# A two-layer graph attention kernel: in layer 1 the edges of the next block are made by GpSimd and the row maxima stay in PSUM

## The chip, the cores and the metric

The kernel runs on one core of one Trainium2 chip. The metric is the device time of one execution in microseconds (us); lower is better. Before the change it is 3500.31 us, the median of 3 runs (3499.39 to 3500.57). TensorE does the matmuls (PE in the profile; PEld are its weight loads), VectorE (DVE) and ScalarE (ACT) the elementwise work, GpSimd (POOL) and SyncE (SP) mainly issue transfers.

## The reference, cut to what matters

There are three attention layers over N = 8192 nodes with C = 64 channels and one 8192x8192 integer adjacency: one in the first residual block, two in the second. Each does, for every row of the adjacency, a masked softmax and a weighted sum of features:

```
e = leaky_relu(u[:, None] + v[None, :] (+ c), 0.2)
scores = where(adj > 0, e, -9e15)
att = softmax(scores, axis=1)
h = elu(att @ features ...)
...
x = layernorm(x + gnn0(x, adj))          # kernel layer 0
x = layernorm(x + gnn1(x, adj))          # kernel layers 1 and 2, then an MLP over [x, h1, h2]
```

The adjacency is read as integers once; the kernel turns it into a byte mask, keeps that mask in device memory and reads it again in layers 1 and 2.

## The kernel before, in words

The program calls its three attention layers l = 0, 1, 2. Each layer is worked in NB = 16 blocks of BI = 512 rows of the adjacency (they lie along the free axis, so everything is transposed), and each block in NT = 64 tiles of 128 columns (they lie on the partitions). The code is written out by hand for each engine: each of them runs the same loop over blocks and tiles, and semaphores hold them together. There is no scheduler; what stands at a tile index `t` in an engine's loop is issued after that engine's work on tile t.

For tile j of a block:
- DVE, `start_scores` (L1156): writes max(ua + v8col[j], cb) into one of ES = 5 score banks `eps` of PSUM. `ua` (128x512) holds the rows' u minus their maxima, `cb` (128x512) the negative maxima, both in SBUF; `v8col[j]` is a [128, 1] operand. It waits until the bank's last user, ACT five tiles ago, is done.
- PE, `mask_scores` (L754): adds a large negative number to the bank where the mask `nt` says "no edge".
- ACT, `probs` (L577): exp of the bank into `prob`.
- PE, `sums` (L798): sums prob times features into the bank `acc`, two tiles per group in layers 1 and 2.

At fixed tile indices two more pieces of work are threaded into the loop of block b.

The tail of block b-1, T_TURN to T_Y (tiles 8 to 35): PE turns the sums into the bank `misc`, DVE divides, applies the elu and makes the features (L1071 to L1099, ending in `s_h`), PE makes the next layer's products, ACT copies them out, and DVE adds them to the running output at tile 35 (L1121, signalled by `s_y`). GpSimd then issues two stores: `u_d` (L521) and `xy_d` (L524). SP loads `xin` for the next tail and the masks of a later block once the `xy_d` store is complete.

The head of block b+1: the kernel wants the largest v among each row's neighbours. `make_edges` (L1004, DVE) turns a quarter of the mask (16 tiles, 128x2048 int32) into 0/1 in FP8 by an exclusive-or with EDGE_FLIP, four times a block, at tiles T_XOR = 29, 32, 40, 41, into two buffers `edges`. PE counts edges by level of v (`count_edges`, L765, tiles 35 and 43), ACT copies the counts out (tile 45), PE turns them (`turn_counts`, L774, tile 47), DVE finds the maxima (`head`, L1022 to L1048, tiles 51 to 53; fourteen instructions, of which the first waits for the turned counts). PE turns the maxima (L841) and spreads them over all partitions into `misc` (L846, tile 57), ACT copies `misc` to `cb` (`rows_out`, L641), and DVE makes the next `ua` (`add_u`, L1162, tile 63).

PSUM has eight banks: five `eps`, `acc`, `den` and `misc`. In layers 0 and 2 `den` sums denominators; in layer 1 it is unused, since the denominator comes out of a turned sum. All tail and head steps share `misc`.

In layer 1 GpSimd has the two stores of each block and nothing else. The 5 buffers `stage`, in which the adjacency lands in layer 0, are unused in layers 1 and 2.

Of the kernel before, what the change touches and what calls it, by code (L numbers as in the profile page):

```python
# [16 lines left out]
P = 128  # L17
# [22 lines left out]
EDGE_FLIP = 0x38383838  # L40
LEVELS = float(HB * LV - 2)
# [63 lines left out]
def build(nc, x, adj, ent, W0, a0, W12, lin_w, lin_b, attn, mlp_w, mlp_b, out):  # L105
    with ExitStack() as ctx:
# [92 lines left out]
        miscb = misc[:, :].bitcast(BF16)  # L199
# [30 lines left out]
        s_xor = sem("edges_made")  # L230
        s_oneh = sem("levels_on_columns")
# [261 lines left out]
        def _(pool):  # L493
# [43 lines left out]
        def _(act):  # L537
# [60 lines left out]
            def columns_out(l, b):  # L598
                act.wait_ge(s_htt, blk(l, b) + 1)
                nc.scalar.activation(ht[0:C, :], misc[0:C, :], ACT.Copy).then_inc(s_hte, 1)  # L600

            def products_out(l, b, i):

                act.wait_ge(s_om, 4 * blk(l, b) + i + 1)
                if i < 2:
                    v = misc[:, 0:2 * WC].rearrange("p (r w) -> p r w", w=WC)
# [19 lines left out]
                elif l < 2:  # L626

                    act.wait_ge(s_ust, 16 + 16 * blk(l, b))
                    nc.scalar.activation(urow[:, :], misc[0:RT, 0:P], ACT.Copy).then_inc(s_oe, 2)

            def counts_out(l, b):
                act.wait_ge(s_hist, MV * (blk(l, b) + 1))
                nc.scalar.activation(hs[:, :], misc[:, :], ACT.Copy).then_inc(s_hse, 1)  # L633

            def maxima_out(l, b, par):
                act.wait_ge(s_mt, blk(l, b) + 1)
                nc.scalar.activation(mrow[0:3, par, :], miscb[0:3, 0:BI], ACT.Copy).then_inc(s_mte, 1)  # L637
# [18 lines left out]
            for l in range(NLAYER):  # L656
                counts_out(l, 0)
                maxima_out(l, 0, 0)
                rows_out(l, 0, 0)

                def body(b, par, head, tail):
                    for t in range(NT):
# [8 lines left out]
                        if b == 0 and l == 1 and t == T_FSUM:  # L671
                            act.wait_ge(s_fs1, 1)
                            nc.scalar.activation(acc_s[0:C, 0:P], misc[0:C, 0:P], ACT.Copy).then_inc(s_fs1e, 1)
                        if b == 0 and t == T_FSUM + 4:
                            act.wait_ge(s_fsum, l + 1)
                            nc.scalar.activation(fsum[:, :], misc[:, 0:CE], ACT.Copy).then_inc(s_fsume, 1)
# [4 lines left out]
                        if head and t == T_ROWS:  # L681
# [9 lines left out]
        def _(pe):  # L691
# [66 lines left out]
            def count_edges(l, b, m):  # L758

                n = MV * blk(l, b) + m  # L760
                pe.wait_ge(s_xor, n + 1)
                for k in range(MT // 4):
                    for s in range(4):
                        j = 4 * k + s
                        mm = nc.tensor.matmul(misc[s * HB:(s + 1) * HB, :], oneh[:, m * MT + j, :],  # L765
                                              half_block(edges[:, n % 2, :], m, j), start=(m == 0 and k == 0),
# [11 lines left out]
            def feature_sum(l, j):  # L778
                if l == 1:
                    mm = nc.tensor.matmul(misc[0:C, 0:P], feat[:, 1, j, 0:C], ones[:, :], start=(j == 0),  # L780
# [4 lines left out]
                mm = nc.tensor.matmul(misc[:, 0:CE], ones[:, :], feat[:, l % 2, j, :], start=(j == 0),  # L785
# [52 lines left out]
            def turn_maxima(l, b):  # L838
                pe.wait_ge(s_split, blk(l, b) + 1)
                for r in range(RT):  # L840
                    mm = nc.tensor.transpose(miscb[0:3, r * P:(r + 1) * P], parts[:, r, 0:3], identb[:, :])  # L841
                mm.then_inc(s_mt, 1)

            def spread_maxima(l, b, par):
                pe.wait_ge(s_mte, blk(l, b) + 1)
                nc.tensor.matmul(misc[:, :], onesb[:, :], mrow[:, par, :], start=True, stop=True).then_inc(s_cb, 1)  # L846

            def tail_step(l, b, t):
                if t == T_TURN:
# [4 lines left out]
                    for r in range(RT):  # L854
                        if l == 1:
                            mm = nc.tensor.matmul(misc[:, r * CE:(r + 1) * CE], acc_s[:, r * P:(r + 1) * P],
                                                  turnw[:, :], start=True, stop=True)
                            continue
                        nc.tensor.matmul(misc[:, r * CE:r * CE + C], acc_s[:, r * P:(r + 1) * P], halves[:, 0:C],  # L859
                                         start=True, stop=True)  # L860
                        mm = nc.tensor.matmul(misc[:, r * CE + C:(r + 1) * CE], den_s[:, r * P:(r + 1) * P],  # L861
                                              halves[:, C:CE], start=True, stop=True)
                    mm.then_inc(s_gt, 1)
                if t == T_HT:
                    for r in range(RT):
                        mm = nc.tensor.transpose(misc[0:C, r * P:(r + 1) * P], hn[:, r, :], ident[:, :])  # L866
# [426 lines left out]
```

## Time and profile before

| | |
|---|---|
| median of 3 runs | 3500.31 us |
| the profiled execution | 3499.27 us |
| its span | 3497.5 us |
| PE busy | 3203.8 us (92%) |
| DVE busy | 2873.2 us (82%) |
| ACT busy | 2269.0 us (65%) |
| POOL busy | 114.3 us (3%) |
| granted TensorE clock, mean | 0.983 |

A busy share says what part of the span an engine had an instruction in flight. Matmuls are pipelined and their ends are modelled, so a PE that reads 94% busy may still be waiting for a little in front of each instruction. Layer 0 lasts until about 1450 us of the span, layer 1 from there to about 2385 us, layer 2 to the end. In a timeline view the columns are the start in us, the duration of the row in us, engine, line, operation, output and inputs with their shapes, how many instructions the row joins, and in brackets how long the engine had been idle and what released it.

### The profile page before, as it was taken

Reading aid. Unit: us, or ns where it says so; the run is one execution under the profiler, and the core shown is the slowest. Engines: PE = TensorE matmul, PEld = TensorE weight load, DVE = VectorE, ACT = ScalarE, POOL = GpSimd, SP = SyncE. Lnnn points to the kernel's source line nnn. Section 1 sums busy time; section 2 is a strip of 40 time slices with the busy share of each in tenths; the row PEclk is TensorE's granted clock in tenths of the full one; section 3 lists DMA queues with packets and bytes.
Section 4 is the critical chain, followed back from the end, with each engine's and each line's share of the span. In section 5 each row is a group of like instructions: output and inputs, shape, how many; then the busy total and the mean of one; then the engine's idle time right before and its main releaser. Section 6 shows DMA issues by size and latency. Waiting matters only on the chain. (4 is left out here: it accounts for less than half of the span.)

```text
span 3497.5 us, 58252 instructions
## 1 busy us (share of the span) xinstructions
PE 3203.8 (92%) x22959; PEld 1152.7 (33%) x22959; DVE 2873.2 (82%) x5283; ACT 2269.0 (65%) x3933; POOL 114.3 (3%) x138
## 2 busy tenths in 40 slices
PE   1679999999999999799999999988999999999998
PEld 0323333333333333333333333334333333333333
DVE  5468888888888875699999999986888888888886
ACT  0247766676776666377777787773666666666665
POOL 0000000000000000000000000000000000000000
PEclk9989999999999999899999999998999999999999
DMA  8999999999999951222222222112111211221210
GB/s 253 283 348 346 341 329 347 336 333 340 343 333 341 333 180 54 85 85 97 76 100 73 100 73 101 72 61 85 69 72 64 90 71 57 86 82 57 85 33 7
DMA packets 414116, 578.71 MB, mean 165 GB/s; under 512 B 294402, under 2 KB 315010, under 8 KB 389266
## 3 DMA queue, kind: packets, MB, share of 16 engines
q1 hardware_dynamic: 409458, 564.40, 50.2%
q0 software_dynamic: 4384, 10.59, 1.0%
q8 instruction: 180, 2.95, 0.4%
q14 instruction: 94, 0.77, 0.1%
HBM read 430.10 MB, written 77.69 MB: 145 GB/s over the span
## 5 line engine op out<-in xcount | busy, mean ns | idle before, releaser
L1156 DVE SCALAR_TENSOR_TENSOR eps<-ua,v8col,cb 128x512 f32<-128x512 f32 x2800 | 1971.3, 754 | 376.3 <-ACT prob L577 238.9
L577 ACT ACTIVATE prob<-eps,v2col 128x512 f32<-128x512 f32 x2560 | 1628.4, 688 | 692.2 <-PE eps L754 678.9
L798 PE MATMUL acc<-prob,feat 128*64 128x512 f32 x5120 | 1303.3, 605 | 6.6 <-ACT acc_s L585 6.6
L754 PE MATMUL eps<-nt,nbig 128*64 128x512 fp8e4 (+2 forms) x6542 | 994.3, 384 | 114.4 <-DVE eps L1156 110.4
L754 PEld LDWEIGHTS eps<-nt,nbig 128*64 128x64 bf16 (+2 forms) x6542 | 329.8, 104 | 956.0 <-DVE eps L1156 612.5
L798 PEld LDWEIGHTS acc<-prob,feat 128*64 128x64 f32 x5120 | 326.2, 137 | 397.9 <-issue 215.0
L577 ACT ACTIVATE mi<-eps,v2col 128x512 f32<-128x512 f32 x512 | 328.0, 686 | 156.7 <-PE eps L754 152.7
L995 DVE TENSOR_SCALAR mi<-stage 128x1024 uint8<-128x1024 int32 x512 | 352.2, 689 | 62.9 <-DMA stage<-in_adj_dram 62.5
L807 PE MATMUL den<-prob,ones 128*32 128x512 f32 x3072 | 397.0, 604 | 0.0
L798 PE MATMUL acc<-mi,feat 128*64 128x512 f32 x1024 | 264.8, 597 | 0.0
L1004 DVE TENSOR_SCALAR edges<-nt 128x2048 int32<-128x2048 int32 x192 | 234.2, 1220 | 31.1 <-PE misc L765 16.3
L765 PE MATMUL misc<-edges,oneh 128*32 128x512 fp8e4 x3072 | 190.8, 390 | 70.6 <-DVE edges L1004 55.8
L564 ACT ACTIVATE eps<-ub,v8col 128x512 f32<-128x512 f32 x272 | 189.4, 696 | 0.0
L807 PEld LDWEIGHTS den<-prob,ones 128*32 128x32 f32 x3072 | 67.1, 108 | 301.0 <-issue 301.0
L765 PEld LDWEIGHTS misc<-edges,oneh 128*32 128x32 bf16 x3072 | 85.0, 98 | 198.3 <-issue 81.1
L807 PE MATMUL den<-mi,ones 128*32 128x512 f32 x1024 | 123.1, 598 | 0.0
L751 PE MATMUL eps<-mrow,onesb 128*32 128x512 bf16 (+1 forms) x800 | 106.5, 379 | 0.0
L633 ACT ACTIVATE hs<-misc 128x512 f32<-128x512 f32 x48 | 28.3, 589 | 93.8 <-PE misc L765 93.8
L798 PEld LDWEIGHTS acc<-mi,feat 128*64 128x64 f32 x1024 | 68.2, 137 | 54.4 <-issue 20.2
L878 PEld LDWEIGHTS misc<-wcat,ht 65*128 65x128 f32 x384 | 52.5, 198 | 77.8 <-issue 49.5
L637 ACT ACTIVATE mrow<-misc 3x512 bf16<-3x512 bf16 x48 | 28.1, 586 | 76.3 <-PE misc L841 76.3
L878 PE MATMUL misc<-wcat,ht 65*128 65x130 f32 (+1 forms) x384 | 69.8, 306 | 6.5 <-ACT pj L624 4.5
(159 smaller groups left out, 1407.1 us busy)
## 6 DMA issues: line engine op xcount, KB each, us to landing
stage<-in_adj_dram SPq DMA_DIRECT2D x512, 512.0 KB, 6.5
nt<-nt_d SPq DMA_DIRECT2D x128, 1024.0 KB, 5.2
nt_d<-nt SPq DMA_DIRECT2D x64, 1024.0 KB, 7.2
ub<-u_d SPq DMA_DIRECT2D x48, 256.0 KB, 5.2
xy_d<-xin POOLq DMA_DIRECT2D x32, 256.0 KB, 3.3
xin<-xy_d SPq DMA_DIRECT2D x32, 256.0 KB, 2.9
nt<-mi SPq DMA_TRANSPOSE x256, 7.2
xin<-in_x_dram SPq DMA_DIRECT2D x16, 128.0 KB, 6.3
```

Source lines behind the costliest of these rows:

```text
L564: nc.scalar.activation(eps[:, j % ES, :], ub[:, par, :], ACT.Relu, bias=v8col[:, j:j + 1], scale=1.0 - ALPHA).then_inc(s_filla, 1)
L577: nc.scalar.activation(weights(l, j), eps[:, j % ES, :], ACT.Exp, bias=v2col[:, j:j + 1]).then_inc(s_p, 1)
L633: nc.scalar.activation(hs[:, :], misc[:, :], ACT.Copy).then_inc(s_hse, 1)
L751: nc.tensor.matmul(et[c:c + cols, :], onesb[:, c:c + cols], mrow[:, par, :], start=False, stop=False, skip_group_check=True, tile_position ...
L754: mm = nc.tensor.matmul(et[c:c + cols, :], nbig[:, c:c + cols], edge, start=False, stop=True, skip_group_check=True, tile_position=(0, c))
L765: mm = nc.tensor.matmul(misc[s * HB:(s + 1) * HB, :], oneh[:, m * MT + j, :], half_block(edges[:, n % 2, :], m, j), start=(m == 0 and k == 0),
L798: mm = nc.tensor.matmul(acc[h:h + C, :], feat[:, l % 2, j, 0:C], weights(l, j), start=(k == 0), stop=(k == NT // 2 - 1))
L807: mm = nc.tensor.matmul(den[32 * i:32 * i + 32, :], ones[:, 0:32], weights(l, QUAD * k + i), start=(k == 0), stop=(k == NT // QUAD - 1))
L878: mm = nc.tensor.matmul(misc[:, r * WC + w:(r + 1) * WC], ht[:, (2 * i + r) * P:(2 * i + r + 1) * P], wcat[:, l, w:WC], start=True, stop=True)
L995: dv.tensor_scalar(out, src, 0, ONE8, ALU.is_le, ALU.mult).then_inc(s_mask, 1)
L1004: dv.tensor_scalar(edges[:, n % 2, :].bitcast(I32), nt[:, b % 2, m, :].bitcast(I32), EDGE_FLIP, None, ALU.bitwise_xor).then_inc(s_xor, 1)
L1156: dv.scalar_tensor_tensor(eps[:, j % ES, :], ua[:, par, :], v8col[:, j:j + 1], cb[:, par, :], ALU.add, ALU.max).then_inc(s_fill, 1)
```

## The change

Five things change, all for layer 1.

1. The edges of blocks 1 to 15 are made by GpSimd and no longer by DVE. Each quarter is made in EDGE_PARTS = 4 instructions of 128x1024 16-bit elements, as 0x3838 minus the mask, where DVE did one exclusive-or of 128x2048 int32.
2. Quarters 0 and 1 go to the two `edges` buffers, quarters 2 and 3 to the first four `stage` slots, so each quarter of a block has its own buffer.
3. In GpSimd's program the first two quarters stand ahead of a wait for the tail's features (`s_h`), the other two behind it, and the stores `u_d` and `xy_d` of the tail behind both.
4. The maxima stay in PSUM: the blocks of layer 1 use `misc` and `den` in turn (`max_bank`), `start_scores` and `add_u` read the bank, and ACT's copy to `cb` is gone in this layer. The tail and head steps use the other bank (`work_bank`).
5. The waits on the counters follow: PE waits for `s_edge`, and `s_cbe` (now without layer 1's copies) is counted by `copied`.

Block 0 of layer 1 and all of layers 0 and 2 keep their edges on DVE.

```diff
+EDGE_PARTS = 4
+EARLY_EDGES = 2
@@
+        edges1 = stage[:, 0:4, :].rearrange("p s w -> p (s w)").bitcast(U8).rearrange("p (m w) -> p m w", m=2)
@@
+        def max_bank(b):
+            return (misc, den)[b % 2][:, :]
+        def work_bank(l, b):
+            return max_bank(b + 1) if l == 1 else misc[:, :]
+        def by_pool(l, b):
+            return l == 1 and b > 0
+        def edge_buffer(l, b, m):
+            return edges1[:, m - 2, :] if by_pool(l, b) and m >= 2 else edges[:, m % 2, :]
@@ GpSimd
-            for l in range(NLAYER):
-                for b in range(NB):
-                    tail(l, b)
+            def make_edges(b, m):
+                n = MV * blk(1, b) + m
+                sl, count = landed(1, b, m)
+                pool.wait_ge(sl, count)
+                if b > 1:
+                    pool.wait_ge(s_hist, n - MV + 1)
+                elif m < 2:
+                    pool.wait_ge(s_hist, n - 1)
+                w = MT * BI // EDGE_PARTS
+                for i in range(EDGE_PARTS):
+                    nc.gpsimd.tensor_scalar(edge_buffer(1, b, m)[:, i * w:(i + 1) * w].bitcast(U16),
+                                            nt[:, b % 2, m, i * w:(i + 1) * w].bitcast(U16), -1.0,
+                                            float(EDGE_FLIP & 0xffff), ALU.mult, ALU.add).then_inc(s_edge, 1)
+
+            for b in range(NB):
+                tail(0, b)
+            for b in range(NB):
+                for m in range(MV if b < NB - 1 else 0):
+                    if b > 0 and m == EARLY_EDGES:
+                        pool.wait_ge(s_h, blk(1, b - 1) + 1)
+                    make_edges(b + 1, m)
+                if b > 0:
+                    tail(1, b - 1)
+            tail(1, NB - 1)
+            for b in range(NB):
+                tail(2, b)
@@ ScalarE
-                        if head and t == T_ROWS:
+                        if head and t == T_ROWS and l != 1:
                             rows_out(l, b + 1, 1 - par)
@@ TensorE, count_edges
-                pe.wait_ge(s_xor, n + 1)
+                if by_pool(l, b):
+                    pe.wait_ge(s_edge, EDGE_PARTS * (MV * (b - 1) + m + 1))
+                else:
+                    pe.wait_ge(s_xor, MV * (NB + 1 + b if l == 2 else blk(l, b)) + m + 1)
@@ VectorE
+            def maxima(l, b, par):
+                return max_bank(b) if l == 1 else cb[:, par, :]
-                dv.scalar_tensor_tensor(eps[:, j % ES, :], ua[:, par, :], v8col[:, j:j + 1], cb[:, par, :],
+                dv.scalar_tensor_tensor(eps[:, j % ES, :], ua[:, par, :], v8col[:, j:j + 1], maxima(l, b, par),
@@
-                            for m in range(MV):
+                            for m in range(0 if by_pool(l, b + 1) else MV):
                                 if t == T_XOR[m]:
                                     make_edges(l, b + 1, m)
```

DVE's program in a middle block of layer 1, before: from the tiles behind the features to the first instruction of the head.

```order
L1156 SCALAR_TENSOR_TENSOR eps<-ua,v8col,cb 128x512 x9
L1004 TENSOR_SCALAR edges<-nt 128x2048
L1156 SCALAR_TENSOR_TENSOR eps<-ua,v8col,cb 128x512 x3
L1004 TENSOR_SCALAR edges<-nt 128x2048
L1156 SCALAR_TENSOR_TENSOR eps<-ua,v8col,cb 128x512 x3
L1121 TENSOR_TENSOR xin<-xin,pj 128x4x64
L1156 SCALAR_TENSOR_TENSOR eps<-ua,v8col,cb 128x512 x5
L1004 TENSOR_SCALAR edges<-nt 128x2048
L1156 SCALAR_TENSOR_TENSOR eps<-ua,v8col,cb 128x512
L1004 TENSOR_SCALAR edges<-nt 128x2048
L1156 SCALAR_TENSOR_TENSOR eps<-ua,v8col,cb 128x512 x10
L1022 TENSOR_SCALAR he<-misc 128x128
```

The same place in DVE's program of the change (`den` is here the bank that holds the block's maxima, `misc` the work bank):

```order
L1212 SCALAR_TENSOR_TENSOR eps<-ua,v8col,den 128x512 x15
L1174 TENSOR_TENSOR xin<-xin,pj 128x4x64
L1212 SCALAR_TENSOR_TENSOR eps<-ua,v8col,den 128x512 x16
L1074 TENSOR_SCALAR he<-misc 128x128
L1075 SCALAR_TENSOR_TENSOR hx<-he,kstep 128x128
L1076 TENSOR_TENSOR hx<-hx,he 128x128
L1077 TENSOR_REDUCE kmax<-hx 128x4
```

The four `edges` instructions are gone from between the scores, and the scores read a PSUM bank in place of `cb`.

GpSimd's program before, from the last block of layer 0 into layer 1: each block of layer 1 has its two stores. The names in brackets are the semaphores that a row waits for: `next_products_out` is `s_oe`, `output_sums_done` is `s_y`.

```order
L517 TENSOR_TENSOR rstd<-mom,half 128x4 [waits variance_done]
L521 DMA u_d<-urow 4x128 [waits next_products_out]
L524 DMA xy_d<-xin 128x4x128 [waits output_sums_done]
L521 DMA u_d<-urow 4x128 [waits next_products_out]
L524 DMA xy_d<-xin 128x4x128 [waits output_sums_done]
```

GpSimd's program of the change, one block of layer 1 (`mask_loaded0` to `mask_loaded7` are the landings of the mask quarters, 0 to 3 of even and 4 to 7 of odd blocks, `edges_counted` is `s_hist`, `features_done` is `s_h`):

```order
L564 TENSOR_SCALAR edges<-nt 128x1024 [waits edges_counted,mask_loaded0]
L564 TENSOR_SCALAR edges<-nt 128x1024 x3
L564 TENSOR_SCALAR edges<-nt 128x1024 [waits edges_counted,mask_loaded1]
L564 TENSOR_SCALAR edges<-nt 128x1024 x3
L564 TENSOR_SCALAR stage<-nt 128x1024 [waits edges_counted,mask_loaded2,features_done]
L564 TENSOR_SCALAR stage<-nt 128x1024 x3
L564 TENSOR_SCALAR stage<-nt 128x1024 [waits edges_counted,mask_loaded3]
L564 TENSOR_SCALAR stage<-nt 128x1024 x3
L543 DMA u_d<-urow 4x128 [waits next_products_out]
L546 DMA xy_d<-xin 128x4x128 [waits output_sums_done]
```

Sixteen instructions now stand ahead of a block's stores, eight of them behind the wait for the features.

## Rows read from the trace of the kernel before

**Rows 1.** Busy time by stretch: layer 1, layer 2, one block of layer 1. Columns: stretch, length, each engine's busy us, clock, DMA share, GB/s.
```profile
1450.00:2385.00 935.00, 860.28 (x5433) 311.82 (x5432) 861.23 (x1523) 698.92 (x1222) 20.62 (x32) 0.99 0.24 86
2385.00:3497.50 1112.50, 1093.97 (x7641) 401.23 (x7641) 904.38 (x1694) 697.49 (x1167) 40.60 (x32) 0.98 0.17 63
1615.75:1672.61 56.86, 53.41 (x340) 19.11 (x338) 53.98 (x95) 44.09 (x78) 1.28 (x2) 1.00 0.24 89
```

**Rows 2.** Timeline of DVE in that block.
```profile
1615.75 9.37 DVE L1156 SCALAR_TENSOR_TENSOR eps<-ua,v8col,cb 128x512 f32<-128x512 f32 x14
...
1632.27 0.43 DVE L1099 SCALAR_TENSOR_TENSOR hn<-hn,z 128x256 f32<-128x256 f32 x1
...
1638.58 1.22 DVE L1004 TENSOR_SCALAR edges<-nt 128x2048 int32<-128x2048 int32 x1
1639.71 2.08 DVE L1156 SCALAR_TENSOR_TENSOR eps<-ua,v8col,cb 128x512 f32<-128x512 f32 x3
...
1644.82 0.42 DVE L1121 TENSOR_TENSOR xin<-xin,pj 128x256 f32<-128x256 f32 x1
...
1659.73 0.29 DVE L1022 TENSOR_SCALAR he<-misc 128x128 int32<-128x128 int32 x1
```

**Rows 3.** Groups by line, 1505 to 2295 us: count, busy us, mean ns, idle before.
```profile
L1156 DVE SCALAR_TENSOR_TENSOR eps<-ua,v8col,cb 128x512 f32<-128x512 f32 x890 | 609.0, 753 | 31.5 <-ACT prob L577 30.1
...
L1004 DVE TENSOR_SCALAR edges<-nt 128x2048 int32<-128x2048 int32 x56 | 68.3, 1219 | 0.0
...
L1071 DVE SCALAR_TENSOR_TENSOR g<-fsum,emp,misc 128x65 f32<-128x65 f32 x56 | 11.9, 275 | 0.0
...
L1162 DVE SCALAR_TENSOR_TENSOR ua<-ub,cb 128x512 f32<-128x512 f32 x13 | 8.9, 685 | 0.0
...
L1099 DVE SCALAR_TENSOR_TENSOR hn<-hn,z 128x256 f32<-128x256 f32 x14 | 6.0, 426 | 0.5
...
L1030 DVE SCALAR_TENSOR_TENSOR ns<-vm,gst,vucol 128x4 f32<-128x4 f32 x14 | 3.1, 223 | 0.5
```

**Rows 4.** Timeline of PE in that block, in order of time.
```profile
1634.99 1.02 PE L798 MATMUL acc<-prob,feat 128*64 128x512 f32 x4
...
1645.37 1.03 PE L798 MATMUL acc<-prob,feat 128*64 128x512 f32 x4
...
1648.62 1.02 PE L798 MATMUL acc<-prob,feat 128*64 128x512 f32 x4
...
1649.91 1.02 PE L798 MATMUL acc<-prob,feat 128*64 128x512 f32 x4
...
1657.66 1.02 PE L798 MATMUL acc<-prob,feat 128*64 128x512 f32 x4
...
1660.05 1.08 PE L798 MATMUL acc<-prob,feat 128*64 128x512 f32 x4
```

**Rows 5.** Timeline of SP: loads behind the tail's store.
```profile
1648.79 0.37 SPq L385 DMA_DIRECT2D xin<-xy_d  x1
1649.22 23.61 SPq L437 DMA_DIRECT2D nt<-nt_d  x4
```

**Rows 6.** DMA issues, 1648 to 1656 us: KB each, median us to landing.
```profile
nt<-nt_d SPq DMA_DIRECT2D x2, 1024.0 KB, 6.5
```

**Rows 7.** Groups by line on POOL, whole span.
```profile
L499 POOL MEMSET mrow<- 128x1024 bf16 x1 | 1.0, 951 | 0.1
...
L502 POOL TENSOR_SCALAR_AFFINE_SELECT ident<-ident 128x128 f32<-128x128 f32 x1 | 0.3, 290 | 0.2 <-POOL halves L499 0.2
```

**Rows 8.** Timelines of POOL and DVE in layer 0; last, POOL's group in layer 1.
```profile
513.22 1.10 POOL L521 DMA_DIRECT2D u_d<-urow  x1 [13.59 <-ACT urow L629]
...
513.54 0.69 DVE L995 TENSOR_SCALAR mi<-stage 128x1024 uint8<-128x1024 int32 x1
...
L521 POOL DMA_DIRECT2D u_d<-urow x14 | 7.3, 518 | 837.2 <-ACT urow L629 837.2
```

More of the change, by code:

```diff
@@ L311, in freed, with copied @@
             return tile(l, b, last) - NT + 1
+        def copied(l, b):
+            return b + 1 if l == 0 else NB + b + 1
         def den_blocks(l, b):
@@ L599, in columns_out @@
                 act.wait_ge(s_htt, blk(l, b) + 1)
-                nc.scalar.activation(ht[0:C, :], misc[0:C, :], ACT.Copy).then_inc(s_hte, 1)
+                nc.scalar.activation(ht[0:C, :], work_bank(l, b + 1)[0:C, :], ACT.Copy).then_inc(s_hte, 1)
             def products_out(l, b, i):
@@ L764, in count_edges @@
                         j = 4 * k + s
-                        mm = nc.tensor.matmul(misc[s * HB:(s + 1) * HB, :], oneh[:, m * MT + j, :],
-                                              half_block(edges[:, n % 2, :], m, j), start=(m == 0 and k == 0),
+                        mm = nc.tensor.matmul(wb[s * HB:(s + 1) * HB, :], oneh[:, m * MT + j, :],
+                                              half_block(eb, m, j), start=(m == 0 and k == 0),
                                               stop=(m == MV - 1 and k == MT // 4 - 1), skip_group_check=True,
@@ L779, in feature_sum @@
                 if l == 1:
-                    mm = nc.tensor.matmul(misc[0:C, 0:P], feat[:, 1, j, 0:C], ones[:, :], start=(j == 0),
+                    mm = nc.tensor.matmul(work_bank(1, 0)[0:C, 0:P], feat[:, 1, j, 0:C], ones[:, :], start=(j == 0),
                                           stop=(j == NT - 1))
@@ L784, in feature_sum @@
                     return
-                mm = nc.tensor.matmul(misc[:, 0:CE], ones[:, :], feat[:, l % 2, j, :], start=(j == 0),
+                mm = nc.tensor.matmul(work_bank(l, 0)[:, 0:CE], ones[:, :], feat[:, l % 2, j, :], start=(j == 0),
                                       stop=(j == NT - 1))
@@ L845, in spread_maxima @@
                 pe.wait_ge(s_mte, blk(l, b) + 1)
-                nc.tensor.matmul(misc[:, :], onesb[:, :], mrow[:, par, :], start=True, stop=True).then_inc(s_cb, 1)
+                nc.tensor.matmul(work_bank(l, b - 1), onesb[:, :], mrow[:, par, :], start=True, stop=True).then_inc(s_cb, 1)
             def tail_step(l, b, t):
+                wb = work_bank(l, b + 1)
                 if t == T_TURN:
@@ L927, in body @@
                             pe.wait_ge(s_fs1e, 1)
-                            nc.tensor.matmul(misc[:, 0:CE], acc_s[0:C, 0:P], turnw[0:C, :], start=True,
+                            nc.tensor.matmul(work_bank(1, 0)[:, 0:CE], acc_s[0:C, 0:P], turnw[0:C, :], start=True,
                                              stop=True).then_inc(s_fsum, 1)
@@ L1003, in make_edges @@
                     dve.wait_ge(s_hist, n - 1)
-                dv.tensor_scalar(edges[:, n % 2, :].bitcast(I32), nt[:, b % 2, m, :].bitcast(I32), EDGE_FLIP, None,
+                dv.tensor_scalar(edge_buffer(l, b, m).bitcast(I32), nt[:, b % 2, m, :].bitcast(I32), EDGE_FLIP, None,
                                  ALU.bitwise_xor).then_inc(s_xor, 1)
@@ L1071, in tail_aggregate @@
                     ins = dv.scalar_tensor_tensor(g[:, r, :], fsum[:, :], emp[:, par, r:r + 1],
[L1072 removed]
+                                                  work_bank(l, b + 1)[:, r * CE:(r + 1) * CE], ALU.mult,
+                                                  ALU.add)
                 step(ins, seq, at + 1)
```

50 lines of the change are left out of this document (27 added, 23 removed).

## Prediction

> **What bounds the kernel now.** I read the busy time by stretch first. In layer 1, the only layer that the change touches, 935 us hold 860 us of PE and 861 us of DVE; in layer 2 PE is busy for 1094 of 1112 us and DVE for 904 [rows 1]. So layer 2 is PE's alone, and layer 1 is shared. One block of layer 1 takes 56.86 us with 53.41 us of PE, 53.98 of DVE and 44.09 of ACT [rows 1]. A busy PE is not PE at its peak, so the two have to be counted by their spacing.
>
> DVE, from its timeline in the block: 14 scores in a row take 9.37 us with the last one 0.75 long, so they follow each other every (9.37 - 0.75) / 13 = 0.663 us [rows 2], shorter than the 753 ns of one, since they overlap [rows 3]. 64 of them are 42.4 us. One `edges` instruction moves the next score by 1639.71 - 1638.58 = 1.13 us [rows 2], four are 4.5 us. DVE idles ahead of scores for 31.5 us over 14 blocks [rows 3], 2.3 a block. The rest of 56.86 is tail and head, 7.7 us.
>
> PE, from its timeline: where nothing holds it, a group of two tiles (masks and sums) takes 1649.91 - 1648.62 = 1.29 us [rows 4]; 32 groups are 41.3. A group that DVE holds takes 2 x 0.663 = 1.33. Counting two quarters of edges adds 1648.62 - 1645.37 - 1.29 = 1.96 us, twice a block, 3.9. Turning the counts adds 1660.05 - 1657.66 - 1.29 = 1.10. The middle of the tail, six groups, takes 1645.37 - 1634.99 = 10.38, which is 2.6 over six plain ones [rows 4]. Turning the sums, and the two steps of the maxima together, I put at 1.1 each like the counts. The sum is 51.1 us.
>
> So DVE needs 54.6 us of the 56.9, PE 51.1: DVE is the bound of layer 1, by a little.
>
> **The change part by part.** Edges off DVE: 4.5 us a block, in 15 blocks (those whose next block is in layer 1 as well). DVE then needs 50.1, PE 51.1, and PE becomes the bound. The two don't meet smoothly: DVE is at most five banks ahead, that is five tiles or 3.3 us, and its work in the head comes as one piece. I add 1.2 us for what PE still waits: 52.3 us a block if GpSimd disturbs nobody. That is 4.5 us saved in each of 15 blocks, 68 us.
>
> Maxima in PSUM: ACT loses one 128x512 copy a block, ACT has 12 us of a block idle [rows 1], nothing. At the layer's start one such copy leaves the path, some 0.6 us. What matters is whether a score that reads PSUM in place of `cb` takes longer. Two instructions of one form with SBUF operands give the slope: (685 - 426) / 256 = 1.01 ns an element and 167 ns fixed. The 65-element one that reads `misc`, with a [128, 1] operand, has 275 - 66 = 209 fixed; the 4-element one that reads SBUF, also with a [128, 1] operand, 223 - 4 = 219 [rows 3]. So reading PSUM costs between 10 ns less than SBUF and, if the whole of 209 - 167 is its doing, 42 ns more. I take nothing, since the pair with the same kind of operand is the nearer; the upper end is 64 x 0.042 = 2.7 us a block.
>
> The rule of the Trainium skill that speaks against this edit is in "VectorE: DVE Perf Modes", on the errata: a VectorE instruction with its source in PSUM has 120 fixed cycles where SBUF has 58. By it each score would lose an estimated 62 cycles, 0.065 us, and a block 4.1 us, nearly all that the edges give. The rows above don't show such a difference, though none reads and writes PSUM at once.
>
> GpSimd's time for a part: the trace has no `tensor_scalar` of POOL. The nearest rows are a memset of 128x1024 16-bit elements, 951 ns, and a 128x128 select with input and output, 290 ns [rows 7]. Below, 0.95 us is the floor; above, the select's whole time scaled by eight, 2.3 us. I take 1.03 us with the gap to the next, because the select read and wrote and its 290 ns are mostly fixed. A quarter of a block is then 4.1 us and half a block 8.2.
>
> Late half: the features end at 1632.27 + 0.43, 17 us into the block [rows 2]. Eight parts end at 25.2. The output sum at tile 35 comes at 29.1 now [rows 2] and, two edges earlier, near 26.8, so the stores behind it wait for nothing new. PE counts these quarters at tile 43, over 8 us later still. Free.
>
> Early half: it stands at a block's beginning in the program, but what it waits for is the landing of the masks, and SP asks for those behind the store of `xin`. In the block shown the output sum is at 1644.82, SP's load of `xin` at 1648.79, the first two mask quarters go out at 1649.22 [rows 2, 5] and land 6.5 us later [rows 6], at 1655.7. GpSimd has nothing else by then, so the early half runs there, 10.9 us after the output sum, and not at the next block's beginning. The head begins at 1659.73 [rows 2], 4.0 us behind that start, when PE has turned the counts. With DVE further ahead of PE, the output sum moves some 1.3 us forward against it: 5.3 us. So of 8.2 us, 2.9 still lie in front when the head begins, three parts.
>
> Do they disturb each other? Of the head's fourteen instructions all but `he` (it reads PSUM) and the reduction work on SBUF tiles alone. POOL's store at 513.22 took 1.10 us, where the same takes 518 ns in layer 1; DVE had one 0.69 us instruction in flight from 513.54 to 514.23, and POOL's ended 0.09 behind it [rows 8]. So an instruction of one engine can hold the other's for its whole length. In "SBUF — State Buffer" the Trainium skill says so as a rule (section "SBUF: two separate sides"): DVE and GpSimd share a pair of ports, DVE takes it with two SBUF inputs or in a two-port mode, and whoever has it keeps it for the whole instruction. The rows show POOL held by DVE; that DVE is held by POOL is the other half of the rule and stands in no row.
>
> I take the scores, which now have an operand in PSUM, to be clear of the parts, and the tail lies between the halves. The head's twelve instructions within SBUF I take to be held: each can wait for the part in flight, and three parts cost 0.5 + 1.0 + 1.0 = 2.5 us, less 0.3 that the PE waits anyhow, 2.2 us. PE has only four tiles in hand there, and the head without this already uses them up, so 2.2 us are late on PE too. Bounds: nothing (no holding, or the early half over in time) and all eight parts in the head, 8 us.
>
> **Sum.** 52.3 + 2.2 = 54.5 us a block in place of 56.86, 2.36 saved, in 15 blocks 35 us; with the layer's start 35.6. Against the profiled execution of 3499.3 us that is 3463.7, and the median stands 1 us above it: 3465 us.
>
> **The rivals.**
>
> A, no disturbance: GpSimd and DVE don't meet, or only briefly. Each block 52.3, 68 us less: 3432. For it: the scores are kept clear, and POOL held by DVE is all that rows show. Against it: the order of landing and head above.
>
> B, the parts are slow and the head is held; slower than before. If a part takes 1.4 us with its gap, the late half ends at 28.2 and delays the stores by 1.4; the early half begins 3.9 us ahead of the head and lasts 11.2, so 7.3 us or five parts lie in it. The head grows by 4.5 x 1.4 = 6.3, less 0.3, and the output sum is held once by 0.7. 52.3 + 6.7 = 59.0, 2.1 us more than now, in 15 blocks 32: 3532. At 1.6 us it is nearly seven parts and some 3590. The point from which it decides is a head delay of 4.9 us, which a part of about 1.3 us gives. For it: the part computes two operations with a change of type, the memset none. Against it: the memset's rate at exactly this size. "GPSIMD Engine Reference" of the Trainium skill (section "Elementwise — side-by-side cycle accounting") has 1.8 cycles an element as a good rate, an estimated 1.54 us for a part, and that would make B true; its section "Engine selection" calls one-input operations roughly line rate, which would be my 1.0.
>
> C, scores from PSUM cost more: with 42 ns DVE needs 52.8, the block 54 without and 56.2 with the held head, 10 us saved; with a little more the change is nil. 3498, no change.
>
> **How the numbers follow.** Forecast 40%, A 20%, B 28%, C 12%. The forecast's own range is 3442 to 3484, from a head delay of 1 to 3.7 us. The range for 8 in 10 reaches from just under A to the slower part of B: 3427 to 3540. Within 0.2% (7 us, about what a measurement can tell) lie C and the seam between forecast and B. Faster 0.60, same 0.12, slower 0.28.
>
> **What would show it.** In the profile after: DVE without `edges` in layer 1 blocks 0 to 14; scores still every 0.66 us; a group on PE at 1.29 us nearly throughout; POOL with 240 parts of about 1 us, the early eight starting about 11 us behind the output sum. In the head, DVE instructions that are longer or start later than now, next to a POOL part. Layers 0 and 2 as long as before. I am wrong if the parts run at 1.3 us or more (then B), if the scores' spacing is above 0.69 (then C), or if the head takes as long as now with parts beside it (then A). It is also wrong if the landing of the masks moves so that the early half meets the tail's instructions at tiles 13 to 20.

## The result, and the profile after

The change takes 3520.68 us (median of 4 runs, 3518.87 to 3523.31), the kernel before 3499.85 us (4 runs on the same chip, 3497.85 to 3500.57). The ratio is 1.0062, with a 95% interval of 1.0048 to 1.0076: slower by 0.6%, 21 us. The forecast was 3465 us, faster.

One block of layer 1, for the kernel after (columns as in [rows 1]):

```profile
1621.41:1680.08 58.67, 53.85 (x341) 19.67 (x338) 51.65 (x92) 43.77 (x77) 18.06 (x18) 0.97 0.24 86
```

The block lasts 58.67 us, where it took 56.86 [rows 1]. DVE is busy for 2.3 us less in it and the block is 1.8 us longer. Its clock is 0.97; in [rows 1] it was 1.00.

Timeline of DVE in the head of that block:

```profile
1663.65 0.29 DVE L1074 TENSOR_SCALAR he<-misc 128x128 int32<-128x128 int32 x1
1663.98 1.12 DVE L1075 SCALAR_TENSOR_TENSOR hx<-he,kstep 128x128 f32<-128x128 int32 x1
1665.13 1.09 DVE L1076 TENSOR_TENSOR hx<-hx,he 128x128 f32<-128x128 f32 x1
1666.26 0.29 DVE L1077 TENSOR_REDUCE kmax<-hx 128x4 f32<-128x128 f32 x1
1666.58 0.65 DVE L1078 TENSOR_SCALAR emp<-kmax 128x4 f32<-128x4 f32 x1
...
1670.31 4.70 DVE L1212 SCALAR_TENSOR_TENSOR eps<-ua,v8col,den 128x512 f32<-128x512 f32 x7
```

Timeline of POOL there:

```profile
1637.35 8.91 POOL L564 TENSOR_SCALAR stage<-nt 128x1024 uint16<-128x1024 uint16 x8 [28.84 <-DVE hn L1152]
1648.86 0.57 POOL L543 DMA_DIRECT2D u_d<-urow  x1 [2.60 <-ACT urow L675]
...
1658.30 8.91 POOL L564 TENSOR_SCALAR edges<-nt 128x1024 uint16<-128x1024 uint16 x8 [8.10 <-DMA nt<-nt_d]
```

The edges are off DVE and eight parts take 8.91 us on GpSimd. The late half runs from 1637.35 to 1646.26 and holds up no store: the first one behind it then waits 2.60 us for its own input. The early half begins at 1658.30, the head at 1663.65, and the half ends at 1667.21. Three instructions of the head that take 0.29, 0.29 and 0.17 us alone (the run `e2_early_behind_head` below shows them) last 1.12, 1.09 and 0.65. `he`, which reads PSUM, and the reduction `kmax` are as short as ever with a part in flight. From `he` to the row of seven scores it is 1670.31 - 1663.65 = 6.66 us.

The trace has fifteen heads in layer 1. In the first and the last no part is in flight, and they take 4.54 us each. The other thirteen meet the early half, which begins 3.1 to 5.8 us ahead of them, and take 6.17 to 8.09 us, 88.0 us together.

Timeline of PE in the same stretch:

```profile
1668.92 0.41 PE L801 MATMUL eps<-nt,nbig 128*64 128x512 fp8e4 x2 [2.58 <-DVE eps L1212]
1669.98 0.41 PE L801 MATMUL eps<-nt,nbig 128*64 128x512 fp8e4 x2 [0.65 <-DVE eps L1212]
1670.22 1.82 PE L849 MATMUL acc<-prob,feat 128*64 128x512 f32 x4
1671.83 1.07 PE L801 MATMUL eps<-nt,nbig 128*64 128x512 fp8e4 x4
1672.68 1.55 PE L849 MATMUL acc<-prob,feat 128*64 128x512 f32 x4
```

And the windows of 3 us over it:

```profile
1665.40:1668.40 3.00, 0.95 (x6) 0.06 (x2) 2.79 (x8) 1.24 (x2) 1.74 (x2) 1.00 0.17 71
1668.40:1671.40 3.00, 1.83 (x8) 0.55 (x10) 2.86 (x9) 1.38 (x2) 0.00 (x0) 0.82 0.00 0
1671.40:1674.40 3.00, 3.00 (x11) 0.76 (x7) 3.00 (x6) 1.27 (x2) 0.00 (x0) 0.61 0.00 0
```

PE waits 2.58 and 0.65 us for the held scores. After that its groups of four `acc` matmuls last 1.82 and 1.55 us in place of 1.02, and the granted clock (the third value from the right) is 0.82 and 0.61: in them TensorE runs partly at 1.2 GHz and not at 2.4. In the next window it is 1.00 again. Behind each of the thirteen held heads at least one such group lasts 1.8 us or more; behind the two free ones none lasts more than 1.08.

### The profile page after: what moved, and what is told of

The parts are those of the page before. It is cut to its first block and busy times, and to the rows that moved or that the text cites. A ratio compares the mean times of both kernels' runs of the same rounds, so it can differ in the third digit from the quotient of the medians.

```text
span 3519.0 us, 58303 instructions
## 1 busy us (share of the span) xinstructions
PE 3194.7 (91%) x22848; PEld 1160.9 (33%) x22959; DVE 2838.2 (81%) x5223; ACT 2265.6 (64%) x3917; POOL 365.7 (10%) x378
## 5 line engine op out<-in xcount | busy, mean ns | idle before, releaser
L1212 DVE SCALAR_TENSOR_TENSOR eps<-ua,v8col,cb 128x512 f32<-128x512 f32 x1776 | 1268.6, 754 | 319.1 <-ACT prob L623 183.9
L849 PE MATMUL acc<-prob,feat 128*64 128x512 f32 x5120 | 1318.4, 611 | 7.0 <-ACT acc_s L631 7.0
L1212 DVE SCALAR_TENSOR_TENSOR eps<-ua,v8col,misc 128x512 f32<-128x512 f32 x512 | 349.7, 749 | 64.4 <-ACT prob L623 63.3
L1212 DVE SCALAR_TENSOR_TENSOR eps<-ua,v8col,den 128x512 f32<-128x512 f32 x512 | 347.7, 749 | 45.5 <-ACT prob L623 44.7
L816 PE MATMUL misc<-edges,oneh 128*32 128x512 fp8e4 x2336 | 148.1, 397 | 70.8 <-DVE edges L1056 56.0
L1056 DVE TENSOR_SCALAR edges<-nt 128x2048 int32<-128x2048 int32 x132 | 161.0, 1219 | 30.2 <-PE misc L816 16.5
L564 POOL TENSOR_SCALAR stage<-nt 128x1024 uint16<-128x1024 uint16 x120 | 125.4, 1045 | 409.3 <-DVE hn L1152 400.9
L564 POOL TENSOR_SCALAR edges<-nt 128x1024 uint16<-128x1024 uint16 x120 | 125.7, 1047 | 173.4 <-DMA nt<-nt_d 102.3
L539 POOL TENSOR_TENSOR rstd<-mom,half 128x4 f32<-128x4 f32 x16 | 23.1, 1444 | 1095.5 <-DVE mom L1112 1095.5
L549 POOL TENSOR_TENSOR rstd<-mom,half 128x4 f32<-128x4 f32 x16 | 23.0, 1437 | 1051.3 <-DVE mom L1112 1051.3
L816 PEld LDWEIGHTS misc<-edges,oneh 128*32 128x32 bf16 x2336 | 68.0, 100 | 165.5 <-issue 63.7
```

The costliest lines, as they stand in the source:

```text
L564: nc.gpsimd.tensor_scalar(edge_buffer(1, b, m)[:, i * w:(i + 1) * w].bitcast(U16), nt[:, b % 2, m, i * w:(i + 1) * w].bitcast(U16), -1.0, ...
L816: mm = nc.tensor.matmul(wb[s * HB:(s + 1) * HB, :], oneh[:, m * MT + j, :], half_block(eb, m, j), start=(m == 0 and k == 0), stop=(m == MV ...
L849: mm = nc.tensor.matmul(acc[h:h + C, :], feat[:, l % 2, j, 0:C], weights(l, j), start=(k == 0), stop=(k == NT // 2 - 1))
L1056: dv.tensor_scalar(edge_buffer(l, b, m).bitcast(I32), nt[:, b % 2, m, :].bitcast(I32), EDGE_FLIP, None, ALU.bitwise_xor).then_inc(s_xor, 1)
L1212: dv.scalar_tensor_tensor(eps[:, j % ES, :], ua[:, par, :], v8col[:, j:j + 1], maxima(l, b, par), ALU.add, ALU.max).then_inc(s_fill, 1)
```

## The experiments

The kernel before, run beside each of these, had medians of 3499.3 to 3500.2 us.

### 1. The PSUM part of the change alone

```diff
 def by_pool(l, b):
-    return l == 1 and b > 0
+    return False
```

(GpSimd's loop over quarters is emptied with it, and PE's wait counts DVE's edges again.)

> The maxima stay in PSUM and the banks alternate, but all edges are made by DVE as before. Theory (the head is held by GpSimd's early half and nothing else costs): 3496 to 3501 us, scores still every 0.66 us, block of layer 1 at 56.3 to 56.9 us. Rival (scores that read PSUM, or the alternating banks, cost the time): 3510 us or more, scores' spacing above 0.69 us.

Measured: 3486.37 us (3485.28 to 3487.10), ratio 0.9961 [0.9946, 0.9976]; a block takes 55.90 us. A miss for the theory and the rival: with all its edges back on DVE the kernel is 14 us faster than before. So scores from PSUM cost nothing, and the part that I had counted at 0.6 us is the larger gain of the two.

### 2. The early half behind the head

```diff
 for m in range(MV if b < NB - 1 else 0):
+    if b > 0 and m == 0:
+        pool.wait_ge(s_split, blk(1, b) + 1)
```

> The change, with one more wait: GpSimd's early half of the edges starts only when DVE has finished the head of the same time (maxima_split). Theory (hold of the head, then TensorE idle in one piece and its clock lower): head instructions back at 0.16 to 0.3 us, granted clock 1.00 throughout a block, block at 52 to 53.5 us, 3435 to 3455 us. Rival (GpSimd's 16 parts a block, or the moved stores, cost wherever they stand): 3510 to 3525 us.

Measured: 3478.02 us (3477.59 to 3478.88), ratio 0.9937 [0.9920, 0.9954], with experiment 3 the fastest version. The head and the clock are as expected; the block and the time miss their ranges, the time by 23 us. Its timeline of DVE at the head:

```profile
1657.85 0.29 DVE L1076 TENSOR_SCALAR he<-misc 128x128 int32<-128x128 int32 x1
1658.17 0.29 DVE L1077 SCALAR_TENSOR_TENSOR hx<-he,kstep 128x128 f32<-128x128 int32 x1
1658.50 0.29 DVE L1078 TENSOR_TENSOR hx<-hx,he 128x128 f32<-128x128 f32 x1
...
1659.15 0.17 DVE L1080 TENSOR_SCALAR emp<-kmax 128x4 f32<-128x4 f32 x1
...
1662.40 6.81 DVE L1214 SCALAR_TENSOR_TENSOR eps<-ua,v8col,den 128x512 f32<-128x512 f32 x10
```

Its block, and its timeline of PE at the head:

```profile
1615.00:1670.36 55.36, 52.41 (x340) 19.31 (x338) 49.45 (x92) 43.73 (x77) 18.05 (x19) 1.00 0.25 91
```

```profile
1661.01 0.41 PE L803 MATMUL eps<-nt,nbig 128*64 128x512 fp8e4 x2 [0.46 <-DVE eps L1214]
1662.07 0.41 PE L803 MATMUL eps<-nt,nbig 128*64 128x512 fp8e4 x2 [0.66 <-DVE eps L1214]
...
1663.86 0.41 PE L803 MATMUL eps<-nt,nbig 128*64 128x512 fp8e4 x2 [0.25 <-DVE eps L1214]
```

The head takes 1662.40 - 1657.85 = 4.55 us in place of 6.66, the clock is 1.00, and the block is 55.36 us in place of 58.67.

### 3. All edges in the late half

```diff
-EARLY_EDGES = 2
+EARLY_EDGES = 0
```

> The change with EARLY_EDGES = 0: all four quarters are made behind the tail's features, the stores behind them. Theory: the head is clear, DVE's output sum at tile 35 is held once (about 1 us), the stores leave some 6 us later and the mask landings with them, to nobody's harm: 3440 to 3465 us. Rival (16 parts cost wherever they stand): 3510 to 3525 us. Rival (the later stores and mask loads matter): above 3480 us with PE or GpSimd waiting for mask landings.

Measured: 3479.08 us (3477.91 to 3479.61), ratio 0.9940 [0.9925, 0.9955]; a block takes 55.36 us. The time is that of experiment 2, so two different orders that keep the parts out of the head agree. As there, the gain was expected too large.

### 4. One instruction a quarter

```diff
-EDGE_PARTS = 4
+EDGE_PARTS = 1
```

> The change with EDGE_PARTS = 1: a quarter is one GpSimd instruction of 128x4096 elements, about 4.2 us. Theory (a DVE instruction within SBUF waits for the whole GpSimd instruction in flight): the head's first such instruction lasts up to 4 us where it lasts 1.1 in the change, the head is later by 2 us or more against the change, 3535 to 3580 us. Rival (the engines share the port piece by piece): hold and time like the change, 3515 to 3525 us.

Measured: 3518.15 us (3517.31 to 3518.89), ratio 1.0052 [1.0037, 1.0067]. The time is in the rival's range and not in the theory's, but the rival's mechanism, sharing piece by piece, is not what the trace shows. POOL, then DVE:

```profile
1663.12 7.28 POOL L564 TENSOR_SCALAR edges<-nt 128x4096 uint16<-128x4096 uint16 x2 [7.97 <-DMA nt<-nt_d]
```

```profile
1668.59 0.29 DVE L1074 TENSOR_SCALAR he<-misc 128x128 int32<-128x128 int32 x1
1668.92 1.61 DVE L1075 SCALAR_TENSOR_TENSOR hx<-he,kstep 128x128 f32<-128x128 int32 x1
1670.57 0.29 DVE L1076 TENSOR_TENSOR hx<-hx,he 128x128 f32<-128x128 f32 x1
```

GpSimd's instruction ends at 1670.40, the held one of DVE at 1670.53, and the next is as short as alone. One instruction is held until the other engine's has ended. Over the layer the same DVE line lasts 0.29 to 2.71 us, by how much of GpSimd's instruction is left. The time was expected too high because only this one instruction of a head is held and those behind it go free: the thirteen heads that meet a part take 6.15 us on average, a hold of 1.6 us, where the change has 6.77 and 2.2.

### 5. A delay in the head without GpSimd

```diff
+for i in range(2 if l == 1 and b > 0 else 0):
+    pad = stage[:, 4, :].bitcast(F32)
+    step(dv.tensor_tensor(pad, pad, pad, ALU.add), s_pad, 2 * (b - 1) + i + 1)
```

(on top of experiment 2, ahead of `he`)

> The change with the early half behind the head, and two more DVE instructions (128x1024, in SBUF, meant to last 2.4 us together) in front of each head in layer 1, with no GpSimd part beside them. Theory (what hurts in the change is only that the head is late, and TensorE behind it idle in one piece and then at a lower clock): a block lengthens by more than the 2.4 us, by some 3.5, the granted clock in the head falls below 1.00 as in the change, 3525 to 3535 us. Rival (GpSimd's parts slow other work as well, and the lower clock is theirs): a block lengthens by 2.4 us at most, clock 1.00, 3505 to 3515 us.

Measured: 3537.47 us (3535.67 to 3538.93), ratio 1.0108 [1.0093, 1.0123]. It is 2.5 us above the theory's range and far from the rival's. Against experiment 2 a head costs (3537.47 - 3478.02) / 15 = 3.96 us for 2.5 us of added work. PE in it:

```profile
1676.29 0.41 PE L804 MATMUL eps<-nt,nbig 128*64 128x512 fp8e4 x2 [2.98 <-DVE eps L1218]
...
1677.67 1.92 PE L852 MATMUL acc<-prob,feat 128*64 128x512 f32 x4
```

The slow matmuls come without a GpSimd part beside the head. They follow TensorE's idle, not GpSimd.

### 6. Scores from SBUF beside GpSimd's parts

```diff
-return max_bank(b) if l == 1 else cb[:, par, :]
+return cb[:, par, :]
```

(on top of experiment 2, with ACT's copy to `cb` and its waits put back)

> The change with the early half behind the head, but ACT copies the maxima to SBUF again and the scores and ua read that copy. Theory (a DVE instruction with two inputs in SBUF waits for the GpSimd part in flight): while a half is being made each score waits up to 1.1 us, scores of 1.0 us and more beside parts, some 8 us longer blocks, 3550 us or more. Rival (scores are not held, they write PSUM): the block lengthens only by the copy, 3486 to 3495 us.

Measured: 3637.68 us (3636.38 to 3639.94), ratio 1.0397 [1.0379, 1.0414]; a block takes 66.47 us. The group of scores, this kernel and then the one of experiment 2 (there the scores of the blocks whose maxima lie in `den`):

```profile
L1213 DVE SCALAR_TENSOR_TENSOR eps<-ua,v8col,cb 128x512 f32<-128x512 f32 x763 | 664.8, 943 | 47.5 <-ACT prob L625 46.2
```

```profile
L1214 DVE SCALAR_TENSOR_TENSOR eps<-ua,v8col,den 128x512 f32<-128x512 f32 x468 | 317.5, 750 | 37.2 <-ACT prob L625 36.5
```

A score with two inputs in SBUF is held by the parts (up to 1534 ns for one), one with an input in PSUM isn't (757 ns at most). The parts are held too: eight of them take 11.57 us beside such scores, where they take 8.91. That is what the PSUM edit buys: without it the same edges on GpSimd cost 3637.68 - 3478.02 = 160 us, some 10 of them for the copy itself (experiment 7).

### 7. The PSUM scores with ACT's copy kept

```diff
-    if l != 1:
-        rows_out(l, 0, 0)
+    rows_out(l, 0, 0)
```

(on top of experiment 1: ACT copies every block's maxima to `cb` again and `ua` waits for it, while the scores read PSUM)

> Edges on DVE, scores read the maxima in PSUM as in the first experiment, but ACT still makes the copy (nobody reads it) and ua waits for it. Theory (the gain of the PSUM maxima is the copy's 0.6 us on the way from the head to the next block): 3494 to 3498 us. Rival (the gain is that scores run faster from PSUM): 3485 to 3488 us.

Measured: 3495.82 us (3492.33 to 3499.03), ratio 0.9989 [0.9980, 0.9999]. This is in the theory's range. So of the 13.8 us of experiment 1 some 9.5 are ACT's copy and what hangs on it. Where it costs them, lines of ACT, DVE and PE at the end of a block of the kernel before show:

```profile
1669.35 0.60 ACT L641 ACTIVATE cb<-misc 128x512 f32<-128x512 f32 x1 [0.50 <-PE misc L846]
...
1670.56 1.42 DVE L1156 SCALAR_TENSOR_TENSOR eps<-ua,v8col,cb 128x512 f32<-128x512 f32 x2 [0.88 <-ACT prob L577]
1671.89 0.69 DVE L1162 SCALAR_TENSOR_TENSOR ua<-ub,cb 128x512 f32<-128x512 f32 x1
...
1674.09 0.41 PE L754 MATMUL eps<-nt,nbig 128*64 128x512 fp8e4 x2 [0.26 <-DVE eps L1156]
```

`ua` does not wait for the copy: it starts 1.94 us behind the copy's end, and DVE never idled ahead of it in 13 blocks [rows 3], nor in this experiment. But ACT works in its program's order. It waits 0.50 us for the spread maxima and copies for 0.60, and the `prob` behind, whose end frees a bank for DVE, is later by that. DVE idles 0.88 us for it, and a group of PE at the next block's start takes 2.02 us in place of 1.29. With the copy kept the same waits are there (0.91 us on DVE, a group of 1618.60 - 1616.60 = 2.00 us on PE); in experiment 1 both are gone, and the block is 56.63 - 55.90 = 0.73 us shorter.

The remaining 4.3 us are left for the scores and the alternating banks, which no run separates: 14 scores in a row of experiment 1 last 9.31 us, so they follow each other every (9.31 - 0.75) / 13 = 0.658 us, where it was 0.663 in [rows 2].

### 8. The head in four pieces

```diff
 head: part 0 = he, hx, hx, kmax, emp (tile 51)
+      part 1 = vm, ns, nm, nm        (tile 52, apart from part 0)
```

(on top of experiment 2, in layer 1; the other two pieces move one tile back)

> The change with the early half behind the head, and the head's first nine DVE instructions split over tiles 51 and 52 in place of 51 alone (the others at 53 and 54). Theory (PE's remaining loss against its own 51 us is that DVE's tail and head come as lumps longer than PE's four tiles in hand): PE's idle time behind the head shrinks by 0.5 to 1 us a block, 3463 to 3472 us. Rival (PE's count of 51 us was too low and lumps cost nothing): 3476 to 3480 us.

Measured: 3480.81 us (3476.99 to 3481.38), ratio 0.9944 [0.9929, 0.9959]; a block takes 55.35 us. PE's waits there are now 0.90 and 0.71 us, 1.61 together, against 0.46, 0.66 and 0.25, 1.37 together. The theory fell, and the time is the rival's: cutting DVE's work finer takes nothing off what PE waits. My reading, which no run tests, is that tile by tile DVE needs 0.658 us and PE 1.29 / 2 = 0.645, so DVE cannot win back a lead there.

### 9. Half the delay

```diff
-for i in range(2 if l == 1 and b > 0 else 0):
+for i in range(1 if l == 1 and b > 0 else 0):
```

> The early half is behind the head, as in the run at 3478.02 us, and in layer 1 each head after the first gets one VectorE addition of 128x1024 (1.25 us) ahead of its first features, where the longer experiment had two (2.5 us, 3.96 us a block, and a granted clock of 0.58 in one window of 3 us). Theory (a delay costs itself, and on top some 1.2 to 1.4 us once TensorE's idle at the head is long enough for the clock to fall): TensorE's largest idle at the head becomes about 1.3 + 0.6 = 1.9 us; if the clock stays at 1.00 there, 15 x 1.25 = 19 us, 3497 us (3492 to 3502); if it falls, 15 x 2.6 = 39 us, 3517 us. I take the first, at 0.6. Rival (the delay is partly absorbed by the tiles that TensorE has in hand): under 15 us, below 3492 us.

Measured: 3511.09 us (3509.87 to 3513.99), ratio 1.0036 [1.0022, 1.0050]. This lies between the two values, of which I took the wrong one: the clock falls in ten of the fifteen heads. The run holds its own comparison, two heads of this one kernel. PE at the one:

```profile
2013.65 0.41 PE L804 MATMUL eps<-nt,nbig 128*64 128x512 fp8e4 x2 [1.72 <-DVE eps L1218]
2014.72 0.41 PE L804 MATMUL eps<-nt,nbig 128*64 128x512 fp8e4 x2 [0.66 <-DVE eps L1218]
2014.96 1.02 PE L852 MATMUL acc<-prob,feat 128*64 128x512 f32 x4
```

and at the next:

```profile
2070.28 0.41 PE L804 MATMUL eps<-nt,nbig 128*64 128x512 fp8e4 x2 [1.72 <-DVE eps L1218]
2071.34 0.41 PE L804 MATMUL eps<-nt,nbig 128*64 128x512 fp8e4 x2 [0.66 <-DVE eps L1218]
2071.58 1.53 PE L852 MATMUL acc<-prob,feat 128*64 128x512 f32 x4
...
2073.75 1.83 PE L852 MATMUL acc<-prob,feat 128*64 128x512 f32 x4
```

with their windows:

```profile
2014.00:2017.00 3.00, 2.09 (x14) 0.72 (x14) 2.93 (x7) 2.02 (x4) 1.68 (x2) 1.00 0.01 3
...
2071.00:2074.00 3.00, 2.66 (x12) 1.04 (x14) 2.93 (x8) 1.52 (x3) 2.06 (x2) 0.66 0.00 0
2074.00:2077.00 3.00, 3.00 (x14) 0.59 (x10) 2.37 (x4) 1.64 (x4) 2.76 (x4) 0.77 0.00 0
```

SP's loads of `ub`, one a block, give the price:

```profile
1967.01 0.43 SPq L401 DMA_DIRECT2D ub<-u_d  x1
2023.62 0.43 SPq L401 DMA_DIRECT2D ub<-u_d  x1
2081.44 0.43 SPq L401 DMA_DIRECT2D ub<-u_d  x1
```

The block whose clock stays takes 56.61 us, which is the 55.36 of experiment 2 and 1.25 for the added instruction (1.23 long): here a delay of the head costs itself. The block whose clock falls takes 57.82, 1.2 us more, after the same waits of 1.72 and 0.66 us. From one head to the next the slow groups move: at seven heads in a row the first group of sums lasts 1.92, 1.92, 1.92, 1.73, 1.52, 1.31 and 1.07 us and the second 1.02, 1.23, 1.44, 1.64, 1.85, 1.92 and 1.92, and at the two heads behind them both last 1.02. So the wait alone doesn't decide it; what does, no run shows.

### 10. Parts half as long

```diff
-EDGE_PARTS = 4
+EDGE_PARTS = 8
```

> The change with its edges cut in eight parts of 512 columns for each of the two halves, instead of four of 1024; nothing else. Theory (VectorE's instructions of the head are held until the GpSimd instruction at work has ended, with the held ones alternating with parts): a part takes some 0.52 us plus a fixed 0.07, the three or four held instructions of a head wait 0.3 us each on average instead of 0.7: the head is held for 1.0 to 1.4 us instead of 2.1, and TensorE's idle there falls from 2.6 to about 1.7 us, with the clock of that window back at or near 1.00. Then 3483 to 3500 us, against 3520.68. Rival 1 (more parts, more holds: VectorE is held by each of twice as many parts in turn, the sum stays 2.1 us and the clock falls as before): 3515 to 3530 us. Rival 2 (the time is set by the total of POOL's work beside the head, not by its grain): as rival 1, and the run with one instruction per half (3518.15) speaks for it.

(The eight parts are those of a quarter, as the edit has it, so an early half is sixteen.)

Measured: 3511.20 us (3508.61 to 3513.11), ratio 1.0031 [1.0018, 1.0045]. Between the theory and its rivals: 9.5 us are won, where I expected 20 to 38. A part of half the size takes 622 ns, where 520 and 70 fixed were expected, so the early half is longer (11.21 us), and more instructions of the head meet a part. In a head of the same stretch it is 6.12 us from `he` to the seven scores, PE waits 1.36 and 0.99 us, and a window of 3 us still reads a clock of 0.57. The thirteen heads take 6.11 us on average, a hold of 1.6 us. Finer parts reduce the hold and don't end it, and so does one instruction a quarter (experiment 4), with the same mean hold. From the first to the fourteenth of SP's loads of `ub`, 13 blocks, this kernel takes 753.98 us, experiment 4 755.45 and the change 763.87. What makes experiment 4 slower than this one lies ahead of these blocks: its first such load is at 1510.30, and in the two others at 1503.98 and 1503.88.

## Why the prediction was wrong

**What was right.** GpSimd's part was taken at 1.03 us with its gap and takes 8.91 / 8 = 1.11. The early half was put 5.3 us ahead of the head, with three parts left in it: in the block shown it is 1663.65 - 1658.30 = 5.35 us, and 3.56 us of parts. The hold of the head was put at 2.2 us: it is 6.66 - 4.55 = 2.1 there and 88.0 / 13 - 4.55 = 2.2 on average, though in 13 blocks and not in 15. That DVE is held by GpSimd for whole instructions stood in no row before; experiment 4 shows it, as the other half of the rule in "SBUF — State Buffer" (section "SBUF: two separate sides") of the Trainium skill has it. The scores from PSUM were put clear of the parts and at no cost: so they are. The 120 cycles that the Trainium skill has in "VectorE: DVE Perf Modes", on the errata, for a source in PSUM would have cost an estimated 4.1 us a block. The trace shows no such cost: 749 ns a score against 753.

**The step that failed: "PE 51.1, and PE becomes the bound", with "1.2 us for what PE still waits".** It turned 4.5 us of DVE's work into 4.5 us of time. That made 52.3 us of an undisturbed block; it is 55.36 (experiment 2), 3.1 us more. They stood in the trace of before, on PE, in the block that I had read for its spacing:

```profile
1620.70 1.08 PE L798 MATMUL acc<-prob,feat 128*64 128x512 f32 x4 [0.42 <-ACT acc_s L585]
...
1633.42 0.41 PE L754 MATMUL eps<-nt,nbig 128*64 128x512 fp8e4 x2 [0.97 <-DVE eps L1156]
...
1652.88 0.41 PE L754 MATMUL eps<-nt,nbig 128*64 128x512 fp8e4 x2 [0.26 <-DVE eps L1156]
...
1662.89 0.41 PE L754 MATMUL eps<-nt,nbig 128*64 128x512 fp8e4 x2 [0.47 <-DVE eps L1156]
1663.96 0.41 PE L754 MATMUL eps<-nt,nbig 128*64 128x512 fp8e4 x2 [0.66 <-DVE eps L1156]
...
1665.76 0.41 PE L754 MATMUL eps<-nt,nbig 128*64 128x512 fp8e4 x2 [0.26 <-DVE eps L1156]
```

Of PE's waits in this block only the 0.26 us at 1652.88 are behind edges, and another 0.26 us at 1617.22 are behind ACT's copy (experiment 7). Those shown belong otherwise to the copy of the sums (0.42), to the tail's features (0.97) and to the head (0.47, 0.66, 0.26), 2.78 us together. They are still there when the edges are gone: experiment 2 has 0.47 at the copy of the sums, 0.96 at the features and 0.46, 0.66 and 0.25 at its head.

By the spacing of the sums, in which the prediction counted PE's work, such a place costs more than the wait itself. In experiment 2's block the copy of the sums adds 0.66 us to a plain group, the features 1.15 and the head's two groups 2.00, together 3.8 us, and the other groups another 0.4 in small pieces. With the 51.1 us, whose terms hold, that is the 55.36. I allowed 1.2 for these 4.25.

DVE says the same in the trace of before:

```profile
1657.14 0.76 DVE L1156 SCALAR_TENSOR_TENSOR eps<-ua,v8col,cb 128x512 f32<-128x512 f32 x1 [1.01 <-ACT prob L577]
```

After its last edges and before its head it waits for free banks, so it had caught up with PE, because PE's own counting of edges (twice 1.96 us over a plain group) gives it the time. DVE's edges were for the most part hidden already. Taking them away undisturbed is worth experiment 1 less experiment 2, 8.4 us or 0.5 us a block. On PE it is the one group behind the edges, 1653.12 - 1651.20 = 1.92 us where a plain one takes 1.29. I had booked 4.5 us a block, since I compared two totals (54.6 against 51.1) where the two engines wait for each other by turns, at fixed places.

**The term that was missing: the clock.** A head that is held for 2.1 us leaves PE idle for 2.58 and 0.65 us, and the clock falls behind it, in all thirteen held heads. Experiment 9 prices the fall by itself at 1.2 us, and in the block shown 2.1 + 1.2 = 3.3 us is the difference of 58.67 and 55.36.

**The term that was too small: ACT's copy.** I counted 0.6 us at the layer's start and nothing in the blocks, because ACT has 12 us of idle time in each. But an engine's idle time says nothing of a copy's place in its program: this one, with a wait ahead of it, stands in front of the `prob` that DVE's next score needs. It is worth 9.5 us.

**The account in medians**, from 3500.16 us in the runs of experiment 1: scores from PSUM without the copy, -13.8 (9.5 of it the copy); edges to GpSimd where they disturb nobody, -8.4; the early half beside the head, 3520.68 - 3478.02 = +42.7. These are differences of neighbouring runs, so that they add up to 3520.7 proves nothing; how the last one divides is read from the traces. Over the 13 blocks between the first and the fourteenth load of `ub` the change takes 763.87 us and experiment 2 720.09, 43.8 less. The hold is 88.0 - 13 x 4.55 = 28.9 of it. The rest, 14.9, is 1.15 us a head, and experiment 9 has 1.2 for a fall of the clock.

**The rivals.** A, no disturbance, is experiments 2 and 3, at 3478 and not at 3432. B had the sign right and the cause wrong: the parts aren't slow, and a head delay of 2.1 us is enough where B needed 4.9. That its 3532 comes near the measured time is luck. C, dearer scores, is out by experiment 1. What stays open is why in experiment 9 the clock stays in five heads and falls in the others after the same waits.

## What to carry to other kernels

When two engines work on the same tiles, don't compare their busy sums: list the waits of the one that is to become the bound, with the place and releaser of each, and take away only those that the edit touches. Work given to GpSimd over SBUF can hold VectorE's instructions that work within SBUF, so it belongs beside work with a PSUM operand, and never beside a short serial chain that another engine waits for. A wait on TensorE of 1.7 us or more cost 1.2 us on top by the clock in most heads here, so look at the granted clock behind the longest waits.

## What the runs showed of the hardware

- A VectorE instruction within SBUF that meets a GpSimd `tensor_scalar` is held until that ends: in experiment 4 it ended 0.13 us behind (1670.40 and 1670.53). Even one of 128x4 elements, 0.17 us alone, took 0.65. Scores with the maxima in PSUM (757 ns at most beside parts), `he` (0.29 us) and a reduction (0.29 us) were not held. Where both inputs of a score were in SBUF it was held though it writes PSUM (experiment 6).
- GpSimd's `tensor_scalar` with two operations on 16-bit elements takes 622 ns for 128x512, 1045 for 128x1024 and 3.60 us for 128x4096: 0.83 ns an element and 0.2 us fixed.
- A scores instruction reading PSUM and SBUF and writing PSUM takes 749 ns, 4 less than with both inputs in SBUF.
- After waits of 1.7 and 0.7 us within one head TensorE's clock fell in ten heads of fifteen (experiment 9); in the block shown to 0.66 and 0.77 of full over two stretches of 3 us, at 1.2 us. After 1.2 and 0.7 us it fell in the one head of experiment 4 that has them (groups of 1.51 and 1.86 us). After 0.5 and 0.7 us (experiment 2) and 0.9 and 0.7 (experiment 8) no head has a slow group.
